# State sums of a selective-scan block: TensorE transposes against one strided VectorE reduction

## The reference, cut to what matters

```python
dA = exp(dt[..., None] * A)                         # per token, channel, state
x_scaled = (xb * dt)[..., None] * Bp[..., None, :]
h = scan over tokens of  h = dA * h + x_scaled
y = einsum('bldn,bln->bld', h, Cp) + xb * D_param   # sum over the 16 states, plus x times D
y = layernorm(y) * silu(z);  out = y @ out_w.T
```

## Time and profile before

| | |
|---|---|
| median of 3 runs | 5642.31 us (5641.2 to 5642.68) |
| profiled execution's own time | 5639.12 us |
| its span | 5637.3 us |
| mean granted TensorE clock | 0.889 of full |
| TensorE busy, matmuls | 4983.9 us, 88% of the span |
| VectorE busy | 3802.5 us, 67% |
| ScalarE busy | 3930.8 us, 70% |
| GpSimd busy | 4336.8 us, 77% |

### The profile page before, as it was taken

One profiled execution on the slowest core, in us unless ns is written; L12 is line 12 of the kernel. 1 busy time (PEld: TensorE's weight loads), 2 busy tenths in 40 slices (PEclk: granted clock), 3 DMA queues, 4 the chain that ended last, 5 costly groups with the idle time before them and its releaser, 6 DMA issues.

```text
span 5637.3 us, 91426 instructions
## 1 busy us (share of the span) xinstructions
PE 4983.9 (88%) x31232; PEld 4258.9 (76%) x31232; DVE 3802.5 (67%) x7568; ACT 3930.8 (70%) x9218; POOL 4336.8 (77%) x3272
## 2 busy tenths in 40 slices
PE   4788988989989989999889889889889898899897
PEld 4677777777777777777777777777777777777776
DVE  3667666677677667667667677676666766776763
ACT  4777667677677677676676676676776776776752
POOL 5978778778788787787787787787787787877850
PEclk8789989889889899899899899899898898898887
DMA  4222222222222222222222222222222222222110
GB/s 107 57 45 65 60 53 58 67 54 57 67 54 56 69 49 59 68 51 60 59 60 60 53 66 60 53 63 62 53 58 66 54 57 67 53 56 69 42 36 24
DMA packets 730351, 328.60 MB, mean 58 GB/s; under 512 B 631286, under 2 KB 655136, under 8 KB 729632
## 3 DMA queue, kind: packets, MB, share of 16 engines
q1 hardware_dynamic: 729888, 322.76, 23.5%
HBM read 307.75 MB, written 14.90 MB: 57 GB/s over the span
## 4 chain that ended last, share of the span: by engine, by line
PE 46%; DVE 27%; ACT 16%; issue 8%; POOL 2%; SPq 1%; DMA 0%; DVEq 0%; ACTq 0%; POOLq 0%
PE YB L576 12%; PE G L694 10%; DVE X L1066 9%; PE SB L643 5%; PE G L616 4%; PE SB L653 4%; DVE xbs L1037 4%; PE SB L553 3%; ACT dA L863 3%; ACT dt L844 2%; PE G L608 2%; ACT y L878 2%; PE G L561 2%; ACT xbs L812 2%; PE G L624 1%
## 5 line engine op out<-in xcount | busy, mean ns | idle before, releaser
L1066 DVE TENSOR_TENSOR_SCAN X<-dA,X 128x392 f32<-128x392 f32 x2048 | 1875.6, 957 | 839.1 <-ACT dA L863 805.6
L471 POOL TENSOR_TENSOR X<-X,Cb 128x784 f32<-128x784 f32 x1024 | 1893.8, 1849 | 4.6 <-DVE X L1066 4.2
L461 POOL TENSOR_TENSOR X<-u,Bb 128x784 f32<-128x784 f32 x1024 | 1891.6, 1847 | 4.6 <-DMA Bb<-proj_rows 4.6
L863 ACT ACTIVATE dA<-dt,negA 128x195 f32<-128x195 f32 x4096 | 1517.7, 417 | 272.0 <-DVE X L1066 245.8
L576 PE MATMUL YB<-idn,X 128*98 128x128 f32 x8192 | 1284.6, 311 | 28.9 <-POOL X L471 28.9
L576 PEld LDWEIGHTS YB<-idn,X 128*98 128x98 f32 x8192 | 1077.7, 147 | 166.3 <-issue 107.4
L694 PE MATMUL G<-hg,we 128*128 128x196 f32 x4096 | 772.7, 348 | 5.9 <-DVE hg L1182 5.9
L694 PEld LDWEIGHTS G<-hg,we 128*128 128x128 f32 x4096 | 737.4, 205 | 7.6 <-issue 6.0
L870 ACT ACTIVATE ysb<-YB 98x256 f32<-98x256 f32 x256 | 98.2, 384 | 742.8 <-PE YB L576 692.2
L643 PE MATMUL SB<-km,qm 32*98 32x392 f32 x1024 | 472.2, 588 | 148.9 <-DVE xbs L1045 142.3
L666 PE MATMUL G<-vs,pT 98*98 98x33 f32 x4096 | 406.0, 255 | 125.8 <-DVE att L1130 112.8
(11 more groups left out here) (147 smaller groups left out, 7386.1 us busy)
## 6 DMA issues: line engine op xcount, KB each, us to landing
Bb<-proj_rows SPq DMA_DIRECT2D x256, 392.0 KB, 4.4
Cb<-proj_rows SPq DMA_DIRECT2D x256, 392.0 KB, 3.8
Gb<-gate_rows SPq DMA_DIRECT2D x64, 784.0 KB, 4.7
px<-in_x SPq DMA_DIRECT2D x1024, 36.8 KB
out<-ob SPq DMA_DIRECT2D x64, 196.0 KB
dtin<-proj_rows SPq DMA_DIRECT2D x64, 98.0 KB, 2.8
we<-in_w_e SPq DMA_DIRECT2D x1, 2048.0 KB
proj_rows<-pj SPq DMA_DIRECT2D x64, 25.3 KB
```

The source lines that it names most:

```text
L461: tt(X[(GROUPS * s + g) % RING][:], u[q % 2][:, c:c + 1, :].broadcast_to([P, NG, T]), Bb[:, NG * ng:NG * (ng + 1), :], ALU.mult).then_inc( ...
L471: tt(t[:], t[:], Cb[:, n0:n0 + NG, :], ALU.mult).then_inc(prod_ready, 1)
L863: last = go(dA[i % DRING][:, j, 1:T], dt_[q % 2][:, c, 1:T], ACT.Exp, scale=negA[:, c, n:n + 1])
L1066: v.tensor_tensor_scan(t, dA[i % DRING].rearrange("p n t -> p (n t)"), t, 0.0, ALU.mult, ALU.add).then_inc(scan_done, 1)
```

## The change

The states of two neighbouring groups now share one buffer, a **pair** p (8 pairs per image, two to a chunk, named DUOS in the code). Even pairs have a ninth slab, into which ScalarE writes x times D directly; there is no xD tile. Four such buffers replace the six of before (RING = 4 pairs, so 8 groups). For the pairs 0, 1, 2, 4 and 6, VectorE adds the 8 or 9 slabs in one `tensor_reduce` that reads along the states, 784 bytes apart, and writes 196 sums to a small tile R; TensorE turns R alone, 2 matmuls. For the pairs 3, 5 and 7 TensorE turns all 8 slabs as before, 16 matmuls.

```diff
-RING = 6
+DUOS = GROUPS // 2
+RING = 4
+RRING = 2
+REDUCED = (0, 1, 2, 4, 6)
...
-AT_XD = -12
+AT_XD = (0, 3, 6, 9,)
+AT_RED = (1, 4, 7, 10, 10, 10, 15, 18,)
+AT_SUM = (2, 4, 7, 7, 13, 13, 17, 17,)
...
-AT_Y_OUT = (6, 9, 12, 17,)
+AT_Y_OUT = (6, 11, 15, 18,)
...
+            def reduce_states(s, p):
+
+                dve.wait_ge(prod_ready, GROUPS * s + 2 * (p + 1))
+                if p % 2 == 0:
+                    dve.wait_ge(xD_ready, IC * s + p // 2 + 1)
+                n = len(REDUCED) * s + rank(REDUCED, p)
+                after(dve, taken, n - RRING)
+                v.tensor_reduce(R[(n - 1) % RRING][:], X[p % RING][:].rearrange("p n t -> p t n"), AX_X,
+                                ALU.add).then_inc(reduced, 1)
...
+                if p in REDUCED:
+                    n = len(REDUCED) * s + rank(REDUCED, p)
+                    pe.wait_ge(reduced, n)
+                    rows = [R[(n - 1) % RRING][:]]
+                else:
+                    rows = [X[p % RING][:, j, :] for j in range(slabs(p))]
+                    pe.wait_ge(prod_ready, GROUPS * s + 2 * (p + 1))
+                    if p % 2 == 0:
+                        pe.wait_ge(xD_ready, IC * s + c + 1)
+                for j, row in enumerate(rows):
...
+            def times_d(s, c):
+                if c == 0:
+                    act.wait_ge(S.drained, S.count("xb", s))
+                duo_free(s, 2 * c)
+                go(X[2 * c % RING][:, 2 * NG, :], xbs[s % 2][:, c, :], ACT.Copy, scale=dpar[:, c:c + 1]).then_inc(xD_ready, 1)
```

More of the change, by code:

```diff
@@ L89 @@
 AT_OUT_NORM = 27
[L90 to L92 removed]
+AT_H1T = 27
+AT_H1T_OUT = 31
+AT_MIX = 31
 AT_RK = 32
@@ L165, in live, with rank, slabs @@
     return ((s, (par - slot // GROUPS) % CYCLE),)
+def rank(chosen, p):
+    return sum(x <= p for x in chosen)
+def slabs(p):
+    return 2 * NG + (p % 2 == 0)
 class Bank:
@@ L242, in vit_tower, with states @@
         hT = [sb(f"hT{i}", [P, DC, T]) for i in range(CYCLE)]
-        xbs = sb("xbs", [P, IC, T])
+        xbs = [sb(f"xbs{i}", [P, IC, T]) for i in range(2)]
         pj = sb("pj", [PROJ, T])
         dtin = sb("dtin", [P, T])
-        soft = sb("soft", [P, IC, T])
         dt_ = [sb(f"dt{i}", [P, IC, T]) for i in range(2)]
         u = [sb(f"u{i}", [P, IC, T]) for i in range(2)]
-        xD = [sb(f"xD{i}", [P, IC, T]) for i in range(2)]
         Bb = sb("Bb", [P, STATES, T])
         Cb = sb("Cb", [P, STATES, T])
-        X = [sb(f"X{i}", [P, NG, T]) for i in range(RING)]
+        R = [sb(f"R{i}", [P, T]) for i in range(RRING)]
+        X = [sb(f"X{i}", [P, slabs(i), T]) for i in range(RING)]
+        def states(g, first=0, count=NG):
+            at = NG * (g % 2) + first
+            return X[g // 2 % RING][:, at:at + count, :]
         ysb = sb("ysb", [TB, BLK, INNER])
@@ L488, in at @@
                         return live(b, par, g, slot)
+                    for s, q in at(AT_Y3):
+                        pool.wait_ge(S.drained, S.count("turn_y", s))
+                        pool.wait_ge(S.drained, S.count("z", s))
+                        tt(y3[:], y3[:], zs[:], ALU.mult).then_inc(y3_ready, 1)
+                    for k in range(GROUPS):
+                        for s, q in at(k + 1):
+                            times_c(s, k)
+                    for s, q in at(AT_U):
+                        make_u(s, q)
+                    for s, q in at(AT_KSQ):
+                        pool.wait_ge(where["k"].drained, where["k"].count("k", s))
+                        tt(ka[:], ka[:], ka[:], ALU.mult).then_inc(ksq_ready, 1)
                     for k in range(GROUPS):
@@ L560, in xproj @@
                 for k in range(IC):
-                    last = mm(o[0:PROJ, 0:T], lhsT=wxp[:, k, :], rhs=xbs[:, k, :], start=(k == 0), stop=(k == IC - 1))
+                    last = mm(o[0:PROJ, 0:T], lhsT=wxp[:, k, :], rhs=xbs[s % 2][:, k, :], start=(k == 0), stop=(k == IC - 1))
                 last.then_inc(where["xproj"].filled, 1)
[L564 to L568, removed]
-                    after(pe, y_drained, IC * s + c)
-                    for k in range(BLK):
[L571 to L579, removed]
@@ L764, in step @@
                         mix_keys(s)
-                    for s, q in at(AT_OUT):
-                        project_out(s, q)
-                    for s, q in at(AT_H1T):
-                        pe.wait_ge(where["out"].drained, where["out"].count("out", s))
-                        turn(s, "h1T", h1)
                     for s, q in at(AT_H2T):
@@ L842, in softplus @@
                 after(act, u_ready, s - 1)
+                after(act, xs_pool, GROUPS * (s - 1))
+                soft = u[q % 2]
                 for c in range(IC):
@@ L992, in step @@
                         drain_rk(s)
+                    for n in range(UNITS):
+                        for s, q in at(AT_SCORES[n] + 3):
+                            probs(s, n)
+                    for s, q in at(AT_TANH_X):
+                        tanh_of_x(s)
                     for k in range(GROUPS):
@@ L1214, in step @@
                             attended(s, q, n)
+                    for p in range(PAIRS):
+                        for s, q in at(AT_SCALE[p]):
+                            scale_pair(s, p)
                     for s, q in at(AT_FFN_STATS):
```

270 lines of the change are left out of this document (141 added, 129 removed).

## The result

The changed kernel takes 6524.16 us (median of 4 runs, 6521.21 to 6526.56) against 5641.76 for the one before: 1.156 times as long, interval 1.155 to 1.158. The forecast was 5300.

What follows compares the result with a forecast made beforehand. It took a loop through several engines, TensorE holding the biggest part, to bound the kernel. Per image -5.9 + 3.0 - 2.4 = -5.3 us, 64 times -339, from 5639.1 gave 5300; range 5090 to 5600.

Steps and rivals of the forecast that it cites:

- the three terms of the sum: Per image: -5.9 us for TensorE's transposes, +3.0 for VectorE's reductions, -2.4 for the new order; together -5.3.
- Terms one and two: Per image on the path: fewer TensorE transposes win 5.9 us (bounds 0 to 12.5); VectorE's reductions cost 3.0 (0 to 9.5).
- The reduction's price: On VectorE: 1.94 us per nine-slab reduction, 1.74 for eight slabs, 9.5 us per image, priced from contiguous rows.
- the first rival: VectorE's strided read takes twice the time per element, 3.7 us per reduction, so slower than before, 5857 us; chance 0.15.
- the rival's point of decision: For the slow strided read: from about 3.0 us per reduction, the extra 5.3 us per image eat the gain.
- The rest: x times D, ring and broadcasts of C and B cost nothing more; the new order wins 2.4 us per image.
- The third term: New order: a quarter of ScalarE's 10.8 us per image waiting for YB won, 2.4 us (bounds 2 lost, 9.1 won).
- The rival of VectorE in TensorE's place: Everyone waits for VectorE, all 9.5 us of reductions on the path; gain 0 to 3 us per image, 5639 to 5447; chance 0.14.
- The clock rival: TensorE, with less work, idles more and its clock falls further; 4.2 of 5.3 us per image lost, 5569 us; chance 0.08.
- the sign that the prediction gave for it: TensorE's granted clock below 0.85 in the profile after would show the forecast wrong; 0.87 or above was expected.

Runs made afterwards that it cites:

- f1: The changed kernel's buffers with no pair reduced, every engine's order and all slots those of the kernel before; 5644.68 us.
- e3: The changed kernel with no pair reduced and dt's broadcast issued ahead of the patch loads on Sync's queue; 5861.32 us.
- e5: The changed kernel with its five reductions reading contiguously (wrong numbers summed) and dt's broadcast ahead of the patch loads; 5680.11 us.
- e1: The changed kernel with dt's broadcast issued ahead of the 16 patch loads on Sync's queue, real strided reductions kept; 5921.74 us.
- e2: The changed kernel with no pair reduced, dt's broadcast still behind the patch loads; 6479.86 us.
- f2: f1 with the same five pairs reduced at the real stride, in the order of the kernel before; 6489.07 us.
- e4: The changed kernel with its five reductions reading contiguously (wrong numbers summed), dt's broadcast still behind the patch loads; 6276.27 us.
- e8: The kernel before plus a VectorE tail, GpSimd done: reductions at seven strides and three additions; 8 x 196 took 1.78 us at 4 bytes, 2.92 at 16.
- h2: g3 with ScalarE's copy of chunk 2 one slot later (13 instead of 12); 5341.03 us.
- e7: The kernel before with the patch loads two slots earlier, ahead of dt's broadcast on Sync's queue; 6068.08 us.
- h1: e5 with 9 filler matmuls of constants in slot 2, ahead of the second part of the patches, nothing moved; 5610.69 us.
- f3: The kernel before with 9, 15 and 11 filler matmuls of constants per image ahead of three TensorE waits; 5439.74 us.
- g3: f3 with 6, 12 and 8 filler matmuls instead of 9, 15 and 11; 5346.87 us.
- g1: e5 with 8, 8, 10 and 14 filler matmuls in four slots and three sums of pairs moved; 6513.23 us.
- f4: e1 with each reduction replaced by contiguous additions of SBUF tiles; 6793.29 us.
- g4: f3 with filler transposes (14, 23 and 17) of the same total length instead of matmuls; 5435.6 us.

## Why the prediction was wrong, step by step

The way from before to after, by kernels that differ in one kind of thing each (differences of the medians, rounded):

| step | kernels | us | per image |
|---|---|---|---|
| pairs, ring of four, ninth slab | before to f1 | +3 | 0 |
| new static order, queue mended | f1 to e3 | +217 | +3.4 |
| five reductions at a contiguous price | e3 to e5 | -181 | -2.8 |
| the stride | e5 to e1 | +242 | +3.8 |
| dt behind the patch loads | e1 to after | +602 | +9.4 |
| sum | | +882 | +13.8 |

The steps close, but they don't add in any order. With the queue's stall in place the reductions weigh 44 us (e2), and with strided reductions put in first the way is +3 (f1), +844 (f2), -567 for the new order (e1), +602. Steadiest is dt's place: 602, 619 (e2 to e3) and 596 (e4 to e5) in the new order, 426 in the kernel before.

The forecast, 5300, missed by 1224 us. The queue is 602 of them and the stride 242; the other 380 (e5 against 5300) lie in the three terms of the sum and the clock.

**Terms one and two** (-5.9 for the transposes, +3.0 for the reductions on the path) came out in sum where the price holds: -2.9 per image in the forecast, and -2.8 from e3 to e5. No run parts the two, and the agreement is in part luck: TensorE's busy time fell by 5.6 us per image in that step (357 in all), not by 12.5.

**The reduction's price** failed at the sentence that took 1.01 ns per element from contiguous rows for a read 784 bytes apart. It is the first rival, to which I gave 0.15, with 3.7 us per reduction where 3.39 came. ScalarE's strided read of PSUM, 12% dear, was no guide to VectorE's of SBUF. The Trainium skill's rule (SBUF — State Buffer, section "Door 1: The DMA port swizzle") that a line holds 16 bytes and wants at least two hits agrees with e8: 8 bytes apart, two numbers to a line, is free, 16 pays. The stride's own cost was over-rated: VectorE gained 6.5 us per image by it (e5 to e1, 416 in all) and the time 3.8, where the rival put nearly all on the path. With the real stride the reductions lose 60 us (e3 to e1) instead of winning 181, which would cross at about 3.0 us per reduction, the rival's point of decision; that is luck, since the rival counted 2.4 us of a better order in.

**"The rest"** failed worst. Of Sync's moved work I followed C's and B's broadcasts and priced them at nothing, rightly: GpSimd waited 5.0 us in all for B's in e1, and no wait for C's shows. I left dt's out of the sum without a reason: it moved from slot 5 to 6, the patch loads from 7 to 6, and inside a slot the loads come ahead of it in both kernels. So dt's broadcast, which had been issued ahead of those 16 transfers, 0.52 us each, now comes behind them and behind Sync's wait for TensorE's patches: 602 us, 9.4 per image. The two constants were in the diff, the order and the issue count in the code.

**The third term** (-2.4 for a better order) failed in its mechanism. Where nothing is reduced, the new order costs 3.4 (f1 to e3); beside strided reductions it is worth 567 us (f2 to e1); beside contiguous ones, the price of the forecast, the old order was never run. The argument was ScalarE's wait for YB. It went as forecast, below 300 us, in fact from 711.2 us in f1 to 1.9 in e3, and the time rose by 217 all the same. Of who waited for whom, f1 and then e3:

```profile
ACT ysb L920 <- PE YB L613: 711.2, 131, 9.4
```

```profile
POOL X L504 <- DVE X L1117: 895.1, 571, 4.6
```

GpSimd, whose product now comes first in the slot, stands 895.1 us for scans, 15.8 in f1. That this is what costs the 217 us isn't shown. Moving one copy a slot, at full clock, is worth 0.1 per image (h2), not 2.4.

**The rival of VectorE in TensorE's place** describes the chain after, 33% against 25%. Its own sum was wrong: 9.5 against 5.9 + 2.4 to 5.9 + 5 is between 1.2 lost and 1.4 gained per image, not 0 to 3 gained.

**The clock rival** was right in kind, and the sign that the prediction gave for it, a clock below 0.85, came. But less work on TensorE is only a part of it. With all the transposes left the clock was 0.867 in e3 and 0.819 in e2; taking them away brought it to 0.830 (e3 to e5) and 0.785 (e2 to after). The rest of the fall from 0.889 came with the new order's and the queue's waits (e7, the queue alone, 0.866). In these pairs TensorE's busy time fell by 357 and 379 us, not by 800. What the fallen clock costs in time: h1 won 69 us back in e5, f3 and g3 up to 293 in the kernel before. What the other stretches are worth in e5 is open: g1, meant for it, was confounded, and no run held e5's clock up throughout. Which slots of the new order cost the 217 us is open too.

## What to carry to other kernels

Follow every transfer of a queue that an edit passes, not only the moved one: sixteen cheap issues ahead of a small broadcast on the path made 602 of 882 us. Price a reduction by its stride in bytes, and TensorE's transposes at full clock (18 of them took 2.13 us in f1) before moving them to an engine that needs 3.39. Don't count a wait as won because it goes: look what bounds the period. Where TensorE idles ahead of a wait, look at the granted clock behind it: a few matmuls of constants in three such places (26 per image) made this kernel 5% faster, 35 of them 3.6%.

## What the runs showed of the hardware that I hadn't expected

- VectorE's fp32 reduction of 8 x 196 elements: 1.78 us with the summed numbers 4 or 8 bytes apart, 2.79 to 2.93 at the five strides tried from 16 bytes on, about the same at 16 as at 784.
- Additions of two SBUF tiles beside a busy GpSimd (f4): 2988 ns instead of 0.98 us in e8. A reduction, with one SBUF input, wasn't held up (3385 ns in the kernel, and 2.87 us for its 8-slab form alone against 2.93 in e1). The Trainium skill, SBUF — State Buffer, section "Who interferes with whom", says that a VectorE instruction with two SBUF inputs contends with GpSimd's reads and that `tensor_reduce` never does; these runs agree.
- Transposes kept TensorE's clock up nearly as well as matmuls (g4 0.951, f3 0.982, before 0.889). The rule of the Trainium skill that the prediction weighed (TensorE: Matmul & The Clock Gate, Part 4), that transposes don't count for the clock, isn't borne out here; the measurement decides.
